# Kept value projections, split query and key projections, and half the squares on GpSimd in a fused attention and mixture-of-experts layer

## The reference

```python
xn  = layernorm(x)
qkv = xn @ qkv_w.T + qkv_b                  # 16 heads of 8
a   = softmax(q k^T / sqrt(8)) v            # per batch and head
att = a @ proj_w.T + proj_b
sh  = square(relu(xn @ W_sh_up)) @ W_sh_down        # 128 -> 512 -> 128
p   = sigmoid(xn @ W_router)                         # 8 experts, the best 2, normalised
moe = sum over the 2: weight * (square(relu(xn @ W_up[e])) @ W_down[e])
out = x + att + sh + moe
```

## Time and profile before

| | us |
|---|---|
| median of 3 runs | 460.37 |
| lowest and highest of them | 455.25 and 461.92 |
| the profiled execution | 455.38 |
| its span from first to last instruction | 453.3 |

### The profile page before, as it was taken

One profiled execution on the slowest core, in us unless ns is written; L12 is line 12 of the kernel. 1 busy time (PEld: TensorE's weight loads), 2 busy tenths in 40 slices (PEclk: granted clock), 3 DMA queues, 4 the chain that ended last, 5 costly groups with the idle time before them and its releaser, 6 DMA issues.

```text
span 453.3 us, 12556 instructions
## 1 busy us (share of the span) xinstructions
PE 429.1 (95%) x4354; PEld 340.9 (75%) x4355; DVE 334.2 (74%) x625; ACT 294.5 (65%) x517; POOL 239.8 (53%) x357
## 2 busy tenths in 40 slices
PE   8889768999999999997999999999999999999996
PEld 7877536666666666665999999999999666666664
DVE  8986797898889888986556666566665789888823
ACT  2443546778777877784566666666665767876782
POOL 7081002665556665661477777677777556633320
PEclk9998969999999999997999999999999999999999
DMA  8492202235333552334355555555551433653120
GB/s 227 148 408 82 72 13 72 86 110 163 104 93 125 159 178 84 107 119 131 98 141 147 146 153 153 145 141 140 149 133 41 145 106 105 189 163 94 52 61 25
DMA packets 56323, 56.73 MB, mean 125 GB/s; under 512 B 6514, under 2 KB 46196, under 8 KB 55764
## 3 DMA queue, kind: packets, MB, share of 16 engines
q1 hardware_dynamic: 51060, 41.61, 32.4%
q0 software_dynamic: 4544, 9.35, 6.2%
q10 hardware_dynamic: 672, 5.15, 2.8%
HBM read 26.65 MB, written 16.59 MB: 95 GB/s over the span
## 4 chain that ended last, share of the span: by engine, by line
PE 83%; DVE 11%; issue 3%; ACT 1%; DMA 1%; DVEq 0%; POOL 0%; ACTq 0%; SPq 0%
PE pbank L1451 15%; PE obank L1306 12%; PE sbank L1331 12%; PE fbank L1249 7%; PE fbank L1138 4%; DVE maxes L1002 4%; PE fbank L1140 3%; PE fbank L1139 3%; PE tbank L1138 3%; PE wbank L1278 2%; PE tbank L1140 2%; PE tbank L1139 2%; PE sbank L1443 2%; PE pbank L1138 2%; PE wbank L1285 2%
## 5 line engine op out<-in xcount | busy, mean ns | idle before, releaser
L1002 DVE TENSOR_REDUCE maxes<-sbank 128x4 f32<-128x1024 f32 x128 | 156.7, 1225 | 41.5 <-PE sbank L1331 37.5
L760 ACT ACTIVATE probs<-tbank 128x1024 f32<-128x1024 f32 x128 | 130.8, 1022 | 64.7 <-PE tbank L1336 64.0
L569 POOL DMA_INDIRECT answers<-gathered,block_rows x78 | 84.7, 1086 | 44.0 <-ACT gathered L808 25.3
L538 POOL DMA_INDIRECT tagged<-X,place_of x64 | 62.4, 976 | 27.3 <-PE tbank L1336 14.4
L1451 PE MATMUL pbank<-down_w,probs 128*128 x624 | 76.3, 275 | 0.6 <-ACT gathered L808 0.6
L1331 PE MATMUL sbank<-k_bands,q_bands 31*128 31x256 f32 x512 | 65.1, 331 | 10.4 <-DVE maxes L1002 8.6
L1331 PEld LDWEIGHTS sbank<-k_bands,q_bands 31*128 31x128 f32 x512 | 39.4, 186 | 47.0 <-DVE maxes L1002 36.0
L1451 PEld LDWEIGHTS pbank<-down_w,probs 128*128 128x128 f32 x624 | 73.0, 192 | 0.7 <-issue 0.7
L1306 PE MATMUL obank<-probs,v_ones 128*32 128x256 f32 x1024 | 69.6, 390 | 0.0
L1336 PE MATMUL tbank<-q_bands,k_bands 32*128 32x256 f32 x512 | 64.9, 332 | 0.3 <-ACT probs L760 0.3
L1109 DVE TENSOR_TENSOR block_lo<-block_w,block_hi 128x512 fp32r<-128x512 f32 x39 | 27.0, 691 | 47.2 <-ACT block_hi L793 47.1
(11 more groups left out here) (192 smaller groups left out, 890.9 us busy)
## 6 DMA issues: line engine op xcount, KB each, us to landing
block_w<-in_w_up SPq DMA_DIRECT2D x39, 256.0 KB, 2.8
q_bands<-part_hi SPq DMA_DIRECT2D x32, 128.0 KB
k_bands<-part_hi SPq DMA_DIRECT2D x32, 128.0 KB
tagged<-q_bands ACTq DMA_DIRECT2D x1, 4096.0 KB, 12.2
gathered<-answers SPq DMA_DIRECT2D x16, 256.0 KB, 3.9
gathered<-tagged SPq DMA_DIRECT2D x30, 129.0 KB, 2.2
q_bands<-part_lo SPq DMA_DIRECT2D x16, 128.0 KB
k_bands<-part_lo SPq DMA_DIRECT2D x16, 128.0 KB
```

The source lines that it names most:

```text
L538: pool.indirect_dma_start(out=tagged, out_offset=bass.IndirectOffsetOnAxis(ap=place_of[:, k, tile:tile + 1], axis=0), in_=X[:, tile, :], i ...
L569: pool.indirect_dma_start(out=answers, out_offset=bass.IndirectOffsetOnAxis(ap=block_rows[:, (p - 1) % 4, k:k + 1], axis=0), in_=ys[:, (p ...
L760: nc.scalar.activation(probs[:, j % 4, :], tbank[:], ACT.Exp, scale=SCALE).then_inc(exps_ready, 1)
L1002: nc.vector.tensor_reduce(maxes[:, g // 2, :, 2 * pair:2 * pair + 2, g % 2].rearrange("p t q -> p q t"), sbank[:].rearrange("p (q t k) -> ...
```

## The change

- `route` writes each tile 256 columns wide, two tiles to a bank, in turn to `fbank` and `obank`. ScalarE copies router and value columns (2 x 136) out of each bank (`keep_route`, 16 copies), and TensorE waits for a bank's copy before it writes that bank again. `project_values` and its 96 matmuls are gone. The exponential of the router becomes three, one for each buffer that holds copies.
- `keep_values` moves from VectorE, slot 5, to GpSimd, slot 6, and reads the copies. `add_bias` moves from slot 3 to slot 5 on GpSimd.
- For batches 4 to 15 queries are projected in slot 1 and keys in slot 3, an iteration earlier than before; `high_qk` follows in slots 5 and 6, both low parts in slot 0 of the next iteration (in (9, 7) for batch 12). `project` waits for the low parts of the batch before.
- The first half of the squares moves from ScalarE, slot 2, to GpSimd, slot 3 (`hidden0`). The two halves have buffers of their own, `relu_T` and `relu_T1`.
- `sum_tiles` and `count` are in fp32r. The filling matmuls write to `wbank`.

```diff
+PROJECT = {(c - 2, 1) if c < 3 else (0, 3): (c, (0, 1)) for c in range(4)}
+PROJECT.update({(c - 3, 1 + 2 * qk): (c, (qk,)) for c in range(4, B) for qk in range(2)})
...
-        later = sb("later", [P, 2, TILES * E])
+        later = sb("later", [P, 2, TILES * E], F32R)
         same = sb("same", [P, E])
+        same_once = sb("same_once", [P, E], F32R)
+        sel = sb("sel", [P, 2, P], F32R)
+        chosen = sb("chosen", [P, TILES, E], F32R)
+        tile_sums = sb("tile_sums", [P, 2, P], F32R)
...
+        def v_home(c):
+            w = TT * (E + D)
+            if c < 7:
+                a = block_w[:].rearrange("p r h -> p (r h)")[:, c * w:c * w + w]
+            elif c < 10:
+                a = block_relu[:].rearrange("p r h -> p (r h)")[:, (c - 7) * w:(c - 6) * w]
+            else:
+                a = v_late[:, c - 10, :]
+            return a.rearrange("p (t w) -> p t w", t=TT)
...
+                sp.wait_ge(qk_hi_ready, 2 * c + 2)
...
+                    sp.wait_ge(v_ready, 7)
...
+            nc.gpsimd.tensor_copy(same_once[:], same[:]).then_inc(later_ready, 1)
...
+            def hidden0(c):
+                pool.wait_ge(relu_ready, 2 * c + 1)
+                wait(pool, batch_projected, c)
+                nc.gpsimd.tensor_tensor(hidden_T[:, 0:2, :].rearrange("p c m -> p (c m)"), relu_T[:], relu_T[:],
+                                        ALU.mult).then_inc(hidden0_ready, 1)
+            def keep_values(c):
+                pool.wait_ge(v_kept, c + 1)
+                wait(pool, values_done, (c - 1) * QUADS)
+                nc.gpsimd.tensor_tensor(
+                    v_ones[:, c % 2, :, :].rearrange("p t (h c) -> p t h c", c=VW)[:, :, :, 0:HD],
+                    v_home(c)[:, :, E:].rearrange("p t (h d) -> p t h d", d=HD),
+                    bias_rows[:, 0:D].rearrange("p (h d) -> p h d", d=HD).unsqueeze(1).to_broadcast([P, TT, NH, HD]),
+                    ALU.add).then_inc(v_ready, 1)
...
+            pool.wait_ge(v_ones_set, 2)
+            keep_values(0)
             sent = 0
             for b in range(B):
                 if b < 2:
                     place()
                     pool.wait_ge(slots_zeroed, 32)
                 for j in range(SLOTS):
-                    if b > 1 and j == 3:
-                        add_bias(b)
                     if (b, j) >= FIRST and sent < 2 * TILES:
                         after_scores(b, j)
                         dispatch(sent)
                         sent += 1
+                    if b > 0 and j == 3:
+                        hidden0(b - 1)
+                    if b > 1 and j == 5:
+                        add_bias(b)
+                    if b + 1 < B and j == 6:
+                        keep_values(b + 1)
                     if (b, j) in ADD:
                         add_rows(ADD[b, j])
...
-                    act.wait_ge(logits_ready, CHUNKS)
-                    nc.scalar.activation(table(0).rearrange("p t e -> p (t e)"), fbank[:, 0:TILES * E], ACT.Exp,
-                                         scale=-1.0).then_inc(exp_logits_ready, 1)
-                    act.wait_ge(exp_logits_ready, 1)
+                    act.wait_ge(v_kept, B)
+                    for c0, c1, a in ((0, 7, block_w), (7, 10, block_relu), (10, B, v_late)):
+                        n = (c1 - c0) * TT
+                        a = a[:].rearrange("p r h -> p (r h)")[:, 0:n * (E + D)].rearrange("p (t w) -> p t w", t=n)
+                        nc.scalar.activation(table(0)[:, c0 * TT:c1 * TT, :], a[:, :, 0:E], ACT.Exp, scale=-1.0).then_inc(exp_logits_ready, 1)
+                    act.wait_ge(exp_logits_ready, 3)
                     nc.scalar.activation(table(0), table(0), ACT.Identity, bias=1.0).then_inc(exp_logits_ready, 1)
...
+            def keep_route(c):
+                for h, b in enumerate((fbank, obank)):
+                    act.wait_ge(logits_ready, 2 * c + h + 1)
+                    nc.scalar.activation(v_home(2 * c + h), b[:].rearrange("p (t w) -> p t w", t=TT)[:, :, 0:E + D],
+                                         ACT.Copy).then_inc(v_kept, 1)
+            def high_qk(c, qk):
+                act.wait_ge(qk_projected, 2 * c + 2)
                 wait(act, bands_placed[c % 2], 96 * (c // 2))
-                for qk in range(2):
-                    ins = nc.scalar.activation(part_hi[:, c % 2, qk, :], pbank[:, qk * T:qk * T + T], ACT.Identity,
-                                               bias=bias[:, qk:qk + 1])
-                ins.then_inc(qk_hi_ready, 1)
+                nc.scalar.activation(part_hi[:, c % 2, qk, :], pbank[:, qk * T:qk * T + T], ACT.Identity,
+                                     bias=bias[:, qk:qk + 1]).then_inc(qk_hi_ready, 1)
...
-                    wait(act, hidden1_ready, c)
-                else:
-                    act.wait_ge(hidden0_ready, c + 1)
-                nc.scalar.activation(relu_T[:], fbank[:], ACT.Relu).then_inc(relu_ready, 1)
+                wait(act, (hidden0_ready, hidden1_ready)[n], c)
+                nc.scalar.activation((relu_T, relu_T1)[n][:], fbank[:], ACT.Relu).then_inc(relu_ready, 1)
...
-                    if j == 1 and Q:
-                        high_qk(b + 2)
+                    if j == 1 and b < 1:
+                        for qk in range(2):
+                            high_qk(b + 2, qk)
+                    if j in (5, 6) and (b, 3) in PROJECT:
+                        high_qk(b + 3, j - 5)
...
+                    act.wait_ge(v_ready, 10)
...
-                    if j == 2 and Q:
-                        low_qk(b + 2)
+                    if j == 2 and b < 1:
+                        for qk in range(2):
+                            low_qk(b + 2, qk)
+                    if j == 0 and b > 0 and Q and b != ROUTED_AT + 1:
+                        for qk in range(2):
+                            low_qk(b + 2, qk)
+                    if j == 7 and b == ROUTED_AT:
+                        for qk in range(2):
+                            low_qk(b + 3, qk)
...
-                    if j == 5 and N:
-                        keep_values(b + 1)
...
+                for h, b in enumerate((fbank, obank)):
+                    wait(pe, v_kept, 2 * c + h - 1)
+                    for t in range(TT):
+                        a = (2 * c + h) * T + t * P
+                        cols = slice(a, a + P)
+                        ins = three(b[:, t * WIDE:t * WIDE + WIDE], xT_hi[:, cols], xT_lo[:, cols], w_hi[:, 0:WIDE], w_lo[:, 0:WIDE])
+                    ins.then_inc(logits_ready, 1)
...
-            def project(c):
+            def project(c, parts):
                 pe.wait_ge(xT_lo_ready, c // 2 + 1)
-                wait(pe, v_ready, c - 1)
-                if c == ROUTED_AT + 3:
-                    pe.wait_ge(result_ready, PAIRS)
-                for qk in range(2):
-                    ins = three(pbank[:, qk * T:qk * T + T], wqk_hi[:, qk, :], wqk_lo[:, qk, :], *tokens_T(c))
-                ins.then_inc(qk_projected, 1)
-            def project_values(c):
-                if c + 1 < B:
-                    pe.wait_ge(qk_lo_ready, c + 2)
-                else:
-                    pe.wait_ge(v_ready, c)
-                h, l = tokens_T(c)
-                for t in range(TT):
-                    s = slice(t * P, t * P + P)
-                    ins = three(pbank[:, t * D:t * D + D], h[:, s], l[:, s], wv_hi, wv_lo)
-                ins.then_inc(v_projected, 1)
+                for qk in parts:
+                    wait(pe, qk_lo_ready, 2 * c)
+                    if c == ROUTED_AT + 4:
+                        pe.wait_ge(result_ready, PAIRS)
+                    three(pbank[:, qk * T:qk * T + T], wqk_hi[:, qk, :], wqk_lo[:, qk, :], *tokens_T(c)).then_inc(qk_projected, 1)
...
+                        pe.wait_ge(v_kept, B)
...
-                        if Q:
-                            project(b + 2)
+                        if (b, j) in PROJECT:
+                            project(*PROJECT[b, j])
...
-                        if N:
-                            project_values(b + 1)
+                        if (b, j) in PROJECT:
+                            project(*PROJECT[b, j])
```

78 lines of the change are left out of this document (30 added, 48 removed).

## The result

| | before | after |
|---|---|---|
| median, us | 458.38 (4 runs) | 466.45 (4 runs) |
| profiled execution, us | 455.38 | 467.13 |
| its span, us | 453.3 | 464.7 |
| its mean granted clock | 0.981 | 0.953 |
| ratio to the kernel before | | 1.016 (1.011 to 1.021) |

The changed kernel is 1.6% slower; the forecast was no change. It ran a second time as `a0_again`, unchanged, beside the experiments: 464.67 us, ratio 1.017 (1.008 to 1.026). A ratio compares the undisturbed executions alone, so it can differ from that of the medians. The forecast of 460.1 us was 6.4 us too low, and its range ended at 466.

What follows compares the result with a forecast made beforehand. VectorE's maxima, alternating with scores, were taken to set a 1.82 us slot floor. Terms summed to -0.25 us on the profiled 455.38, giving 455.1; 5.0 to the median made 460.1 us, range 453 to 466.

Steps and rivals of the forecast that it cites:

- The start: Up to the attention: six matmuls and a low-part wait leave, ScalarE's router copies give some back; -1.0 us.
- The counting: Iteration 1: cheaper fp32r products and departing query matmuls save 1.25 us, low parts leaving (1, 2) save 0.75 us.
- The wait in iteration 1: Slot (1, 5): TensorE waits for GpSimd's square, queued behind `place()`'s last copy; +4.2 us.
- The lower clock after it: After iteration 1's wait, TensorE runs 3 to 7 us at half speed once; +2.0 us.
- The attention iterations: Slots 1 and 3 shrink toward VectorE's 1.82 us floor, to 1.93 and 1.83; -3.85 us over the iterations.
- Iteration 10: GpSimd's square comes behind `add_rows(0)`, which waits for gathered rows; +0.5 us net of that iteration's gain.
- Routed blocks: VectorE's low parts of batch 12, in (9, 7), stand ahead of an add that TensorE awaits; +0.25 us.
- The step to the median: Shown runs' median is 5.0 us above the profiled execution; this unexplained difference was carried to the forecast.
- The clock stays up: Rival: no lower clock after iteration 1's wait and the start gains in full, 457.1 us; chance 0.25.
- GpSimd late in every iteration: Rival: GpSimd outruns its 1.6 us of cover, so TensorE waits in slot 5, 470.5 us; chance 0.08.
- The shared port: Rival: VectorE's and GpSimd's squares meet in 14 iterations, showing in slot 4 or 5, +7.0 us, 467.1; chance 0.07.
- TensorE bounds every slot: Rival: all 96 removed matmuls count, 10.6 us in place of 3.85, giving 453.4 us; chance 0.05.

Runs made afterwards that it cites:

- g3_before_busy: The kernel before with SP's order changed in iterations 10 to 15 and 19 matmuls without a use in iteration 0: 455.29 us, ratio 0.993.
- g1_all: Changed kernel with hidden0(0) ahead of placing, both orders exchanged, add_rows behind hidden0(9), SP's order changed, 19 useless matmuls, first squares on GpSimd: 451.03 us, ratio 0.987.
- g2_all_scalar: Same as g1_all but with the first squares on ScalarE, as in the kernel before: 448.46 us, ratio 0.981 to the kernel before.
- g4_busy_only: The changed kernel with only 19 matmuls without a use added in slots 3 to 7 of iteration 0: 463.11 us, ratio 1.010.
- f2_busy: Changed kernel with hidden0(0) ahead of placing, two orders exchanged inside the iteration, and 19 useless matmuls in iteration 0: 456.02 us, ratio 0.992.
- e3_order: Changed kernel with `up` ahead of `project` in slot 1 and `keep_output` ahead of the high part in slots 5 and 6: 461.70 us, ratio 1.004.
- f3_late: Changed kernel with hidden0(0) ahead of placing, two orders exchanged, and iteration 10's first add_rows behind hidden0(9): 454.37 us, ratio 0.988.
- e2_scalar: The changed kernel with the first half of the squares back on ScalarE, behind the relu in slot 2: 457.84 us, ratio 0.988.
- f4_queue: f3_late with the residual's load on SP put behind the stores and gathers in iterations 10 to 15: 455.87 us, ratio 0.988.
- the first four experiments: Changed kernel unaltered, with its square ahead of placing, with squares back on ScalarE, and with two orders exchanged: ratios 1.017, 1.001, 0.988, 1.004.

## Why the prediction failed, step by step

**The start, -1.0, and VectorE's `keep_values` in (0, 5), -0.35: about right together, with the places wrong.** Iteration 1 began 1.34 us sooner in `a0_again` (64.77 against 66.11), but that agrees by luck: the kernel before ran its stretch of 30 to 45 us at a clock of 0.89 and `a0_again` at 1.00. Where the clock is 1.00 in both, iteration 1 begins at 64.80 us in `g3_before_busy` and at 63.77 and 64.02 in `g1_all` and `g2_all_scalar`, 0.8 to 1.0 us sooner. None of it lies ahead of the first exponential (44.16 against 44.08 and 44.32); 0.4 us is in (0, 0), and 0.5 us, VectorE's, shows in (0, 7).

**The counting, -1.25 and -0.75: right.** Slots (1, 1) to (1, 3) gained 2.1 us in `a0_again`, from 9.11 to 7.01, and 1.9 us from `g3_before_busy` to `g4_busy_only`, both with the 19 matmuls. `place()` began 8.71 us into the iteration instead of 9.82, although (1, 0) took 1.0 us more, so the wait moved with the saving, as forecast.

**The wait in iteration 1, +4.2: right, with its length, 4.12 us,** its place behind `place()`'s last copy, and its releaser.

**The lower clock after it, +2.0: right.** In `a0_again` (1, 5) grew by 5.53 us, 1.41 more than the wait, and (1, 6) by 1.39 at the lower level: 2.8 us. In the three other profiles with this wait the same sum is 1.5 us. What the forecast lacked is the clock ahead of the wait: 1.0 us was lost in (1, 0), 3.40 us instead of 2.40. In the first profile the low stretch goes on from 56 to 80 us and takes in the counting itself. I had asked only what clock follows the new wait, not what the time saved ahead of it does to the stretch where TensorE already idled. With the matmuls of `f2_busy` that stretch runs at 1.00. All eight profiles of the changed kernel without them have the long (1, 0); of the kernel before there is one profile, so that the change brings it is likely and not shown.

**The attention iterations, -3.85: the step that failed.** The steady iterations gained nothing (+0.03 us each), and with the waits for the maxima iterations 2 to 8 and 11 to 14 lost 1.95 us; iteration 15 and the rest lost 0.34, its slot 2 falling by 0.33 and its slot 3 growing by 0.32. So a gain of 3.85 us was forecast and a loss of 2.3 us came, 6.1 us apart, nearly the whole distance between the sum of the forecast, -0.25, and the ledger's +6.3. The floor of 1.82 us was right, and slot 3 fell to it. Two of the sentences that followed were wrong, and one slot was missing from them.

*Slot 1: "ends about 1.87 us after its slot began, and is hidden by that".* TensorE's row in the slot 1 that starts at 141.18 us, in the first profile, shows what I had left out:

```profile
142.05 0.36 PE L1184 MATMUL pbank<-xT_lo,w_hi 128*128 128x256 f32 x1 [0.37 <-DVE part_lo L1041]
```

The first of nine matmuls starts 0.87 us after the slot began, at 142.05. The others start 0.20 and then 0.12 us apart, the last at 143.07, and the next scores at 143.28, 2.10 us after the slot began. I had ended my sum at the last matmul and compared it with VectorE's time, when it is TensorE that sets the slot. `e3_order` puts the six matmuls that wait for nothing first: 1.91 us, near the forecast of 1.93.

*Slots 5 and 6: "nothing".* There is room on ScalarE, but it is behind an instruction that TensorE needs. ScalarE's timeline of slot 5:

```profile
150.57 0.47 ACT L763 ACTIVATE part_hi<-pbank,bias 128x256 fp32r<-128x256 f32 x1
150.93 0.39 ACT L770 ACTIVATE out_raw<-obank 128x256 f32<-128x256 f32 x1
```

`keep_output` is now 0.36 us later, and `turn` in slot 6 with it. `e3_order` takes the 0.08 us back.

*Slot 4, not named at all.* With slot 3 shorter, TensorE reaches `turn_attn` before VectorE's normalised rows are there. In iteration 5 they end at 147.42. The last scores of the slot start at 147.16, and in slots 2 and 3 the next work starts 0.21 us behind them, which would be 147.37:

```profile
147.07 0.35 DVE L1072 TENSOR_TENSOR attn<-wbank,recips 128x64 f32<-128x64 f32 x2
147.48 0.44 PE L1328 MATMUL wbank<-ident,attn 128*128 128x128 f32 x2
```

No experiment tried this slot, so it rests on these rows; it is 2.14 us in every profile with the square on GpSimd in which slot 3 is 1.82. A slot that gets shorter hands its slack to the next one.

**Iteration 10, +0.5: too small.** It lost 1.02 us, and the wait was 1.8 (2.2 in the first profile). Over the seven profiles that have this wait it was 1.6 to 2.2 us, and slot (10, 5) stood 1.6 to 3.6 us above its floor, the most where the clock fell behind it (`e3_order` and `g4_busy_only`). I had taken the end of the adds from the trace of before, 9.5 us after the iteration's start; they wait for a gather, and in `a0_again` they end after 10.1 us, with the square 1.0 us behind, while TensorE comes to slot 5 0.3 us sooner. `f3_late` removes 1.8 us in that slot.

**What was in no step: SP's queue.** SP issues the upper maxima of an iteration behind three stores and three gathers, 3.3 us after the start of iteration 14, in the kernel before as in the changed one, and 3.3 us before and 3.95 us in `a0_again` after that of iteration 13. The kernel before did not wait for them there; `a0_again` waited 2.5 us in these two places. Part of the reason is that slot 2 fell from 2.08 to 1.83 us, so that TensorE needs the same DMA sooner: `e2_scalar`, whose slot 2 is at 2.08 again, has slot (14, 3) at 1.91 us instead of 2.54, but (13, 3) still at 2.60. `f4_queue` shows that the queue is what makes them late; why the same place in it was early enough in iteration 13 of the kernel before is open.

**Routed blocks, +0.25: the right kind, too small.** The stretch gained 1.50 us, and two things in it point opposite ways. The first block of the kernel before starts 15.57 us after iteration 9 does, and so it does in `g3_before_busy`; in both profiles of the changed kernel it is 16.2, 0.65 us more. The low parts stand ahead of the add that TensorE awaits, as forecast. VectorE's last add before the blocks in the kernel before:

```profile
207.49 0.42 DVE L1048 TENSOR_TENSOR X<-fbank,resid 128x256 f32<-128x256 f32 x1
```

and VectorE, then TensorE in `a0_again`:

```profile
212.95 0.87 DVE L1041 SCALAR_TENSOR_TENSOR part_lo<-pbank,bias,part_hi 128x256 fp32r<-128x256 f32 x2
213.73 0.42 DVE L1088 TENSOR_TENSOR X<-fbank,resid 128x256 f32<-128x256 f32 x1
...
214.62 0.41 PE L1486 MATMUL sbank<-ident,gathered 128*128 128x128 f32 x2 [1.54 <-DVE X L1088]
```

From there to iteration 10 the kernel before took 144.76 us at its lower clock, `a0_again` 142.60 at 1.00, and the first profile of the changed kernel, at 0.98 like the kernel before, 144.78. So 2.2 us of the ledger are the clock of the blocks, which have no changed line, and without them it would stand at +8.5, near the 8.1 us by which the medians differ.

**The step to the median, +5.0.** I had written that no row says why the median lies above the profiled execution. The list of executions gives most of a reason: the 25 of the kernel before beside the first four experiments go from a span of 453.7 us at a mean granted clock of 0.988 to 462.3 at 0.970, and the longer ones have the lower clocks (correlation -0.75; single ones depart from it, 454.3 us at 0.977 and 458.6 at 0.979). The changed kernel lies at 0.951 to 0.982. So the forecast had to ask how often the clock falls, not only how it stood in one trace.

**The rivals.** *The clock stays up* did not come. *GpSimd late in every iteration* did not either: in the steady iterations nothing waits for its square, as the cover of 1.6 us said. *The shared port* did not show in the steady iterations; it is real in two places, (1, 3) when the square meets the count, and slot 5 of iterations 10 to 14, where it is GpSimd's adds that VectorE's square meets, as in the kernel before. *TensorE bounds every slot* is excluded by busy time that fell by 3.6 us in iterations 2 to 8 while the time rose. The case that came was the mix: my own mechanism in iteration 1, and a gain elsewhere that failed.

## What to carry to other kernels

On an in-order engine the place of a moved instruction matters more than its length: one product behind `place()` cost 5 us, and the same product ahead of it at most the 1.0 us of (1, 3). When a slot gets shorter, list for the next slots each input and what stands ahead of it in its queue, DMA queues too; a gain counts only when the last of them is earlier. And where TensorE idles in a stretch, its clock is a term of its own: look at the spread of clocks over all executions, and fill the idle slots before counting on the full level.

## What the runs showed of the hardware

- The clock can be held up by matmuls without a use. 19 of them in the idle slots of iteration 0 took the mean granted clock of the following 16 us from 0.61 to 1.00, and iteration 1 from 21.16 to 18.01 us. The Trainium skill, page "TensorE: Matmul & The Clock Gate", section "What's actually happening", has activity lift the throttle, and the trace agrees.
- A 128x4 copy on VectorE took 0.98 us beside a 128x512 product on GpSimd and 0.17 us without it.
- GpSimd's product of 128x512 took 1.04 us, as its other product of that size, so an unseen operation was well priced by the nearest row.
